# Forming the convolution kernel inside the input stage, moving two normalisations off VectorE, and loading Toeplitz rows on two queues

## What is computed

```python
x = _ln(idx, n1_w, n1_b)
xg = x @ Wxg
d = _dss(x @ Wdin, n2_w, n2_b, LR, LI, CR, CI, D)
g = d @ Wgate
out = g * xg @ Wout + bout
return out + idx

def _dss(x, n2_w, n2_b, LR, LI, CR, CI, D):
    xn = _ln(x, n2_w, n2_b)
    Lam = (-jnp.exp(LR) + 1j * jnp.exp(LI)).astype(jnp.complex64)
    t = jnp.arange(Lseq, dtype=jnp.float32)
    S = jnp.exp(Lam[:, None] * t[None, :])
    Cc = (CR + 1j * CI) * ((jnp.exp(Lam) - 1.0) / Lam)
    K = jnp.einsum('hn,nl->lh', Cc, S).real
    ... # y = causal convolution of xn with K along the sequence, by FFT
    return y + D * xn
```

## Time and profile before

| | |
|---|---|
| runs | 3219.58 us median of 3 (3217.94 to 3225.70) |
| profiled execution, time | 3219.59 us |
| profiled execution, span in the trace | 3217.8 us |
| VectorE, ScalarE, GpSimd, TensorE busy in the span | 2156.4, 1415.7, 1301.5, 2477.5 us |
| kernel stage | 0.8 to about 46.8 us |
| input stage | about 46.8 to 179.3 us |
| convolution stage | about 179.7 to 270.0 us |

### The profile page before, as it was taken

The page is one execution under the profiler, slowest core; times in us unless marked ns, Lnnn a source line. Parts: engine busy times, 40 slices in busy tenths (PEclk is TensorE's granted clock), DMA queues, the critical chain, the costliest instruction groups (busy, mean ns, idle before and its releaser), DMA issues. The chain is left out here.

```text
span 3217.8 us, 49771 instructions
## 1 busy us (share of the span) xinstructions
PE 2477.5 (77%) x15431; PEld 1752.5 (54%) x15431; DVE 2156.4 (67%) x8218; ACT 1415.7 (44%) x2540; POOL 1301.5 (40%) x2522
## 2 busy tenths in 40 slices
PE   1556873999999999488887699999999622788972
PEld 1424662666656665366665466666666521576751
DVE  5824764787778776388887477777777340467675
ACT  0001320666666666122221266666666401567851
POOL 3310111555555554222221255555655367121166
PEclk9988995899999999699999599999999755799986
DMA  2153002232233221211110322222221341576762
GB/s 32 30 172 95 22 11 34 39 48 42 35 45 47 37 38 32 89 65 51 50 34 4 42 42 35 31 40 42 42 39 25 107 175 58 166 231 218 247 189 74
DMA packets 198792, 229.66 MB, mean 71 GB/s; under 512 B 48621, under 2 KB 148814, under 8 KB 190478
## 3 DMA queue, kind: packets, MB, share of 16 engines
q1 hardware_dynamic: 188302, 207.69, 26.8%
q0 software_dynamic: 8192, 16.79, 1.7%
q10 hardware_dynamic: 2048, 2.10, 0.2%
HBM read 132.55 MB, written 58.10 MB: 59 GB/s over the span
## 5 line engine op out<-in xcount | busy, mean ns | idle before, releaser
L1413 PE MATMUL banks<-Kb,Qb 96*128 96x512 f32 (+3 forms) x2048 | 616.9, 350 | 55.5 <-issue 34.0
L1422 PE MATMUL banks<-Qb,Kb 98*128 98x512 f32 (+1 forms) x1408 | 572.1, 412 | 28.1 <-ACT mha_prob L1314 16.3
L1086 DVE CUSTOM_DVE_ANT_0 mha_junk<-banks,mha_mask 128x512 bf16<-128x512 f32 (+3 forms) x1024 | 453.2, 487 | 186.5 <-PE banks L1413 173.7
L1086 DVE CUSTOM_DVE_ANT_0 mla_junk<-banks,mla_mask 128x512 bf16<-128x512 f32 (+3 forms) x1024 | 454.1, 488 | 161.0 <-PE banks L1413 143.1
L1413 PEld LDWEIGHTS banks<-Kb,Qb 96*128 96x128 f32 x2048 | 372.8, 196 | 303.8 <-DVE mha_nm L1086 100.2
L1314 ACT ACTIVATE mla_prob<-banks 128x512 f32<-128x512 f32 (+1 forms) x704 | 374.8, 559 | 272.7 <-PE banks L1422 271.4
L1314 ACT ACTIVATE mha_prob<-banks 128x512 f32<-128x512 f32 (+1 forms) x704 | 372.6, 559 | 243.0 <-PE banks L1422 239.6
L1209 POOL TENSOR_SCALAR_AFFINE_SELECT mla_prob<-mla_prob 128x128 f32<-128x128 f32 (+2 forms) x704 | 236.7, 347 | 291.6 <-PEq L1421 283.6
L1209 POOL TENSOR_SCALAR_AFFINE_SELECT mha_prob<-mha_prob 128x128 f32<-128x128 f32 (+2 forms) x704 | 237.8, 347 | 269.5 <-PEq L1421 258.2
L1422 PEld LDWEIGHTS banks<-Qb,Kb 98*128 98x128 f32 x1408 | 269.6, 192 | 114.8 <-issue 96.3
L2184 DVE TENSOR_TENSOR moe_hl<-moe_h,moe_hh 128x512 fp32r<-128x512 f32 x212 | 145.7, 689 | 192.3 <-ACT moe_h L2288 102.0
(11 more groups left out here) (436 smaller groups left out, 5104.6 us busy)
## 6 DMA issues: line engine op xcount, KB each, us to landing
moe_wt<-expert_rows SPq DMA_DIRECT2D x53, 1024.0 KB
conv_tz<-conv_kernel SPq DMA_DIRECT2D x16, 1024.0 KB, 6.2
moe_xg<-slots SPq DMA_DIRECT2D x53, 256.0 KB
results<-moe_yt SPq DMA_DIRECT2D x53, 256.0 KB
Kb<-mla_kh SPq DMA_DIRECT2D x32, 256.0 KB, 6.3
Qb<-mla_qh SPq DMA_DIRECT2D x128, 64.0 KB
Kb<-mha_kh SPq DMA_DIRECT2D x32, 256.0 KB, 6.3
Qb<-mha_qh SPq DMA_DIRECT2D x128, 64.0 KB
```

What stands on the lines that cost most here:

```text
L1086: last = dve.tensor_tensor_reduce(junk[:, k % 3, at:at + w], ps[:, bank1(k), at:at + w], mask[:, L - w:L], -1.0, BIG, ALU.add, ALU.min, nm ...
L1413: last = pe.matmul(ps[:, bank1(k), at:at + w], Qb[0:MROW, u, g, h, j * P:(j + 1) * P], Kb[0:MROW, u, g, 0:w], start=True, stop=True)
L1422: pe.matmul(ps[:, bank2(g, k), 0:WIDE[k]].rearrange("p (x w) -> p x w", x=heads), Kb[0:MROW + 2, u, grp, kb * P:(kb + 1) * P], Qb[0:MROW + ...
```

## The change

`kernel_stage` is gone. Its steps are now functions inside the input stage's VectorE program, called after `second_means` of chosen sequences; its loads follow the constants on SyncE, with the four element-wise ones between loads of later sequences. The first normalisation moves to ScalarE, as `Identity` with a column of scales and a column of shifts; GpSimd works out the shifts. The second normalisation moves whole to GpSimd. TensorE transposes sequence n+1 before the products of n. Statistics are now taken two sequences ahead. In the convolution stage the loads of odd groups go through ScalarE's queue, the loops are written out, and the fills of `Kb` and `Qb` stand among GpSimd's copies. The core of the diff:

```diff
-            kernel_stage(nc, io, ps, kd, Qb, Kb)
...
-                    input_stage(nc, io, ps, X, stats, ident, flip, mhalf, U)
-                    convolution_stage(nc, io, ps, U, kd, yd)
+                    input_stage(nc, io, ps, X, stats, ident, flip, mhalf, U, kd)
+                    convolution_stage(nc, io, ps, U, kd, yd, Qb, Kb)
```

The input stage, SyncE and VectorE:

```diff
+                load(0)
                 sp.dma_start(ident[:, :], io["c_ident"]).then_inc(consts, 16)
...
                 sp.dma_start(wd[:, :], io["Wdin"]).then_inc(consts, 16)
+                load(1)
                 sp.dma_start(w2[:, :], rows(io["n2_w"])).then_inc(consts, 16)
                 sp.dma_start(b2[:, :], rows(io["n2_b"])).then_inc(consts, 16)
...
+                for n in range(2, NB):
+                    load(n)
+                    if n == 4:
+                        output_rows(0, crt, io["CR"])
...
+                sp.wait_ge(kpad_ready, 1)
+                sp.dma_start(kd, kpad[:, :]).then_inc(stored, 16)
+                sp.wait_ge(stored, 16)
...
+                for n in range(NB):
+                    low_x(n % 2)
+                    if n + 2 < NB:
+                        means(n + 2)
+                    if n:
+                        second_means((n - 1) % 2)
+                    if n == 1:
+                        decay_rates()
+                    if n == 2:
+                        link(dve.tensor_scalar(ph[:, :], t[:, :], b, None, ALU.mult))
+                        reduce_phase(2048 * 2 * math.pi, 8, 5)
+                    if n == 4:
+                        reduce_phase(2 * math.pi, 12, 3)
+                    if n == 5:
+                        arguments()
+                    if n == 7:
+                        step_decay()
+                    if n == 8:
+                        input_factors()
+                    if n == 10:
+                        coefficients()
+                    if n == 12:
+                        kernel_rows()
```

GpSimd, ScalarE and TensorE in the input stage (`second_means` also waits for `d_done` of two sequences before):

```diff
+                def first_rstd(n):
+                    u = n % 2
                     pool.wait_ge(mv_ready, c.next(mv_ready))
+                    pool.tensor_copy(stats[:, n, :, 0], mv[:, u, :, 0])
+                    chain(pool, c, pdone, pool_rstd(pool, c, pdone, mv[:, u, :, :], var, mhalf, stats[:, n, :, 1]))
+                    chain(pool, c, pdone, pool.tensor_tensor(shift[:, u, :], stats[:, n, :, 0], stats[:, n, :, 1], ALU.mult))
+                    pool.tensor_scalar(shift[:, u, :], shift[:, u, :], -1.0, 0.0, ALU.mult, ALU.add).then_inc(rstd_ready, 1)
+
+                def second_norm(n):
+                    u = n % 2
+                    pool.wait_ge(mv2_ready, c.next(mv2_ready))
+                    chain(pool, c, pdone, pool_rstd(pool, c, pdone, mv2[:, u, :, :], var2, mhalf, rstd2))
+                    for b in range(BLK):
+                        last = pool.tensor_scalar(d[:, u, b, :], d[:, u, b, :], mv2[:, u, b, 0:1],
+                                                  rstd2[:, b:b + 1], ALU.subtract, ALU.mult)
+                    chain(pool, c, pdone, last)
+                    chain(pool, c, pdone, pool.tensor_tensor(
+                        d[:, u, :, :], d[:, u, :, :], w2[:, :].unsqueeze(1).broadcast_to([P, BLK, NC]), ALU.mult))
+                    pool.tensor_tensor(
+                        U[:, :, :, n].rearrange("p h b -> p b h"), d[:, u, :, :],
+                        b2[:, :].unsqueeze(1).broadcast_to([P, BLK, NC]), ALU.add).then_inc(d_done, 1)
+
+                first_rstd(0)
+                first_rstd(1)
+                for n in range(NB):
+                    if n + 2 < NB:
+                        first_rstd(n + 2)
+                    if n:
+                        second_norm(n - 1)
+                second_norm(NB - 1)
...
+                def normalise(n):
                     u = n % 2
+                    act.wait_ge(rstd_ready, c.next(rstd_ready))
+                    for b in range(BLK):
+                        last = act.activation(xh[:, u, b, :], X[:, n, b, :], ACT.Identity, scale=stats[:, n, b, 1:2],
+                                              bias=shift[:, u, b:b + 1])
+                    last.then_inc(xh_ready, 1)
...
+                normalise(0)
+                for n in range(NB):
+                    if n + 1 < NB:
+                        normalise(n + 1)
+                    high_x(n % 2)
+                    if n == 2:
+                        act.wait_ge(a_ready, 1)
+                        act.activation(decay[:, :], t[:, :], ACT.Exp, scale=w[:, 0:1]).then_inc(decay_ready, 1)
+                    if n == WAVES:
+                        act.wait_ge(args_ready, 1)
+                        act.activation(cs[:, :], arg1[:, :], ACT.Sin)
+                        act.activation(arg[:, :], arg[:, :], ACT.Sin).then_inc(waves_ready, 1)
...
+                for n in range(NB):
+                    if n + 1 < NB:
+                        transposes(n + 1)
+                    products(n)
+                    if n == TABLE:
+                        pe.wait_ge(table_ready, 1)
+                        pe.matmul(ps[0:NC, KB, :], coef[:, :], arg[:, :], start=True, stop=True).then_inc(k_ready, 1)
```

The convolution stage, SyncE, GpSimd and ScalarE:

```diff
+                for g in range(0, ALL, 2):
+                    sp.wait_ge(sp_next, c.next(sp_next))
+                    sp.dma_start(tz[:, 0, :, :], lags(g)).then_inc(t_in[0], 16)
...
+                pool.memset(f32(Kb[MROW:P, :, :, :].rearrange("p a g l -> p (a g l)")), 1.0).then_inc(ones_ready, 1)
...
+                    if 4 <= g < 4 + 2 * NG:
+                        pool.memset(f32(Qb[:, (g - 4) // NG, (g - 4) % NG, :, :].rearrange("p h l -> p (h l)")), 0.0)
...
+                for g in range(ALL):
+                    if g % 2:
+                        act.wait_ge(act_next, c.next(act_next))
+                        act.dma_start(tz[:, 1, :, :], lags(g)).then_inc(t_in[1], 16)
+                    if g >= 2:
+                        out(g - 2)
+                out(ALL - 2)
+                out(ALL - 1)
```

More of the change, by code:

```diff
@@ L187, in _, with load @@
[L187 to L189 removed]
+                c = Counts(sp)
+                def load(n):
+                    sp.wait_ge(x_next, c.next(x_next))
+                    sp.dma_start(X[:, n, :, :],
+                                 io["idx"][n].rearrange("(k p) c -> p k c", p=P)).then_inc(x_in[n % 2], 16)
@@ L210, in _ @@
[L210 to L234, removed]
@@ L243, in _ @@
[L243 to L248, removed]
-                link(dve.tensor_copy(kpad[:, KPAD:KPAD + L], ps[0:NC, 0, :]))
@@ L340, in means @@
+                er, ei, dd, u_, wr, wi, p1, p2 = (w[:, n:n + 1] for n in range(1, 9))
+                def means(n):
+                    u = n % 2
                     dve.wait_ge(x_in[u], c.next(x_in[u], 16))
@@ L342, in means @@
                     block_stats(dve, c, done, X[:, n, :, :], st[:, u, :, :], mv[:, u, :, :]).then_inc(mv_ready, 1)
-                def normalise(n, u):
-                    dve.wait_ge(rstd_ready, c.next(rstd_ready))
-                    chain(dve, c, done, dve.tensor_copy(stats[:, n, :, 0], mv[:, u, :, 0]))
-                    for b in range(BLK):
-                        last = dve.tensor_scalar(xh[:, u, b, :], X[:, n, b, :], stats[:, n, b, 0:1],
-                                                 stats[:, n, b, 1:2], ALU.subtract, ALU.mult)
-                    last.then_inc(xh_ready, 1)
                 def low_x(u):
@@ L358, in second_means @@
                     dve.wait_ge(d_ready, c.next(d_ready))
-                    chain(dve, c, done, dve.tensor_tensor(
+                    dve.wait_ge(d_done, c.next(d_done))
+                    link(dve.tensor_tensor(
                         d[:, u, :, :], ps[:, 3 + u, 0:BLK * NC].rearrange("p (b h) -> p b h", b=BLK),
@@ L377, in turn @@
-                def turn(n, u, before, now, after):
-                    if now:
-                        normalise(n, u)
-                    if after:
-                        means(n + 1, 1 - u)
-                    if before:
-                        second_means(1 - u)
-                    if now:
-                        low_x(u)
-                    if before:
-                        second_norm(n - 1, 1 - u)
-                means(0, 0)
-                walk_sequences(dve, c, turn)
+                    block_stats(dve, c, done, d[:, u, :, :], st2, mv2[:, u, :, :]).then_inc(mv2_ready, 1)
```

344 lines of the change are left out of this document (163 added, 181 removed).

## The result

The changed kernel takes 3172.72 us (median of 4, 3169.18 to 3173.73) against 3221.36 (3217.94 to 3225.70) before: 0.9846, 95% interval 0.9829 to 0.9863. The forecast was 3175 us. The profiled execution's span falls from 3217.8 to 3170.4 us, by 47.4.

A forecast was written before the change was run, and what follows sets the result against it. VectorE was taken to pace the old input stage, GpSimd the new one, and even-load waits the convolution pairs. 3219.6 us less 47.9 (input stage, start included) plus 3.0 (convolution) gave 3174.7, stated as 3175; range 3158 to 3197.

The forecast's parts named there:

- The start: Kernel's beginning: VectorE's first work at 8.7 us instead of 52.86 (7.9 if transfers are free, 10 if both are in the way).
- the second loop: Input stage: statistics on VectorE, root on GpSimd, normalisation on ScalarE, low part and next statistics on VectorE; 6.1 us a turn.
- The pace: Input stage after the change: GpSimd's turn, first_rstd 2.0 us plus second_norm 4.8, sets 6.8 us per sequence (5.6 to 8.2).
- The formation's cover: Input stage: the kernel formation's VectorE pieces lie in idle time, except two that lengthen turns to 7.9 and 8.5 us.
- Contention: Rival, slower than before: VectorE and GpSimd obstruct each other in SBUF, GpSimd's turn grows; 3270 us if its operations doubled; chance 0.02.
- The convolution stage: Convolution stage: loads in two queues cost +3 us net; sharing could cost 2 to 11 over seven pairs, staggering could gain.
- the even load's price: Convolution stage: sharing with the odd load in another queue lands the even load 0.3 to 1.5 us later; nothing if queues don't share.
- the even group's 4.2 us at the lower clock: Convolution stage: the even group's 16 matmuls take 4.2 us at clock 0.51, after TensorE idled 4.3 us.
- The rival of the spread groups: Convolution stage: late odd loads shorten TensorE's pauses to 2 us, clock stays up, pairs take 8.35 us; total 3158; chance 0.12.
- the forecast's own sign: Convolution stage: even loads land in 6.2 to 7.7 us, pairs every 10.4 to 11.9; pairs outside that span mean wrong.
- The forecast's cheap bound: Input stage: with four tensor_scalar at their lower bound, 0.6 us, the second loop holds and the last write of U ends at 122.9.
- the rival with 0.07: Input stage: GpSimd is cheap, so the pace is 6.1 us and the total 3167 us; chance 0.07.

## Why the prediction was right, and where its terms were off

- **The start** was 8.7 us; it is 8.52. The first write of U was worked out for 32.7; it ends at 32.70. That is in part luck: the second statistics' root was done at 14.9 us instead of 15.7, the two turns of the second loop took 12.5 instead of 12.2, and the first second_norm 5.4 instead of 4.8.
- **The pace** was 6.8 us with GpSimd as its bound. The bound is right: the turn is its sum, and fell with that sum in the experiments (to 6.41 and 5.46). The size is not. The mis-sized term is the four tensor_scalar: 1.76 forecast, 2.26 measured. The straight line from 128x4 with constants to 128x128 with two columns gave 0.49 for 64 columns; it is 0.59. With 0.798 at 128 columns this leaves, as an estimate, 3.3 ns per column and a fixed 0.38 us, about twice the whole 0.195 of the form with constants. That the column operands are the reason is argued from these rows; no run tried it apart. That and smaller differences (the power at 1.03, unchained starts 0.26 apart) make 0.63 us per turn: 7.6 us in the twelve full turns after the first second_norm and 1.8 in the three short ones.
- **The formation's cover**: forecast as hidden but for two turns. Its VectorE time is, but it stretches what runs beside it, 5.5 us in all, where the forecast had 2.8 (7.9 and 8.5 against 6.8) and that from late statistics. Contention stood in the forecast as a rival only, judged by L1195 in the attention stage. There, for 42 of its 51 us, VectorE runs an instruction that reads one operand from PSUM and one from SBUF. Pace (9.4) and contention (2.6 more than allowed) together make the 12 us by which the stage fell short: 35.9 gained, 47.9 forecast.
- **The convolution stage** was put at +3 and came at -7.7. Two terms failed. One is the even load's price: it was to land 0.3 to 1.5 us later for sharing with the odd load, and landed 0.5 us sooner, by the experiments because the odd load stood behind the stores; that lateness was counted in the forecast only as the point from which the sharing begins. The other is the even group's 4.2 us at the lower clock, which the sum kept for every pair. The rival of the spread groups, with 0.12, is what happened in part: the groups stand apart in three of the eight pairs, and in two of them by its mechanism, with the clock at the upper level. By the forecast's own sign this part was wrong: pairs were to come every 10.4 to 11.9 us with even loads of 6.2 to 7.7, and came every 8.2 to 10.3 with 5.5 to 5.8 after the first. Its other sign held: GpSimd's plain turn stayed between 6 and 8 us.
- **The total** lies 2 us from the forecast because errors of -12 and +11, and 4 us from untouched stages, cancel: the bound of the input stage was understood, the closeness of the number is luck. That the two queues share when issued together is true of the first pair, and costs 1.3 us there.
- **The forecast's cheap bound** for the last write of U, 122.9 us, does not follow from its own terms: the sum that gives 151.6 at the dear end gives 119.8 with 0.6 us for four tensor_scalar and a turn of 6.1. Nothing else hangs on it but the price of the rival with 0.07.

## What to carry to other kernels

Work moved off a full engine is gained only down to the sum of the engine that receives it: add up that engine's turn before the move, and price small instructions by rows with the same kinds of operands: 64 columns with two column operands took three times as long as 4 with constants. A double-buffered load whose latency is as long as the work is a wait in every turn; more buffers take it away, and the next thing to look at is the buffers of the results that share the DMA engines. Work hidden beside another engine's critical chain is not free if it stretches that engine's instructions; here it took back 5.5 of 44 us. And a stage's time can be right by errors that cancel: check its terms, each against the trace.

## What the runs showed of the hardware

- GpSimd tensor_scalar with two column operands: 0.59 us at 128x64, 0.798 at 128x128; tensor_tensor with a broadcast operand 0.64 at 128x256. ScalarE's Identity with a column each for scale and bias: 0.48 us at 128x128, where an activation of that size without took 0.30.
- GpSimd's power of 128x4 took up to 1.46 us instead of 1.01 beside VectorE's scalar_tensor_tensor of 128x512.
- A 1 MB load followed by another 2.2 us later landed in 6.2 us, in one queue or two; followed 2.8 us later in 5.7 in two queues, followed 3.2 us later in 5.5 in one. Two issued together in two queues: the first landed in 7.3 to 7.5, in one queue in 6.1. Why the gap of issue matters was not tried.
- After pauses of 3.0 us TensorE's next group ran at full clock, after one of 2.35 us mostly at the lower level (0.64), both in the same stage: the length of the last pause alone does not tell the clock.
